# Keys of every fourth instead of every second sequence made beside the token list, sources loaded sooner, value units paced by matmul work

## The reference, cut to what matters

```python
topk_w, topk_idx = _route(x, w_router, b_router)          # 4096 tokens, 8 of 64 experts
o = ragged_dot(silu(g) * u, we_down, group_sizes)
y = zeros.at[tok].add(o * w_sorted[:, None])
...
k = keys @ Wk.T + bk;  gk = key_grid @ Wgk.T + bgk         # keys: fside_BxSxS_0, key_grid: ctx_1024
v = values @ Wv.T + bv; gv = key_grid @ Wgv.T + bgv
```

## Time and profile before

| | us |
|---|---|
| median of 3 runs (lowest, highest) | 4605.66 (4602.35, 4606.22) |
| the profiled execution, own time | 4598.36 |
| its span | 4596.7 |
| mean granted TensorE clock, share of full speed | 0.925 |
| prelude of the list (1121 to 1143) | 22 |
| list stage (1143 to 1284) | 141 |
| expert blocks (1284 to 1890) | 606 |
| gather stage of L0_ffn (1890 to 2292) | 402 |

### The profile page before, as it was taken

How to read it: one execution, slowest core, us unless ns; L and a number is a source line. 1 busy time by engine, 2 the same in 40 slices (tenths; PEclk the granted TensorE clock), 3 DMA queues, 4 the chain that set the end, 5 groups by cost and what they waited for, 6 DMA issues and landing times. The chain is left out here.

```text
span 4596.7 us, 96186 instructions
## 1 busy us (share of the span) xinstructions
PE 4050.1 (88%) x32872; PEld 3198.7 (70%) x32872; DVE 2544.2 (55%) x5993; ACT 1849.0 (40%) x3819; POOL 2193.6 (48%) x2362
## 2 busy tenths in 40 slices
PE   6999699965989999688779997999999998499992
PEld 5887577654878888566658774666666665399991
DVE  4665466568944443355546654555555555855553
ACT  2444355533423333211134443555554554155550
POOL 1110322123156666566554534666666664256665
PEclk9999899966999999888889998999999998599996
DMA  1000000001479999777700003332343341166553
GB/s 52 0 0 1 29 12 9 3 29 46 163 228 299 301 299 302 233 240 244 234 12 0 0 1 115 106 105 71 103 106 92 81 106 34 70 221 225 212 205 117
DMA packets 295001, 540.89 MB, mean 118 GB/s; under 512 B 36496, under 2 KB 136976, under 8 KB 283792
## 3 DMA queue, kind: packets, MB, share of 16 engines
q1 hardware_dynamic: 154128, 340.87, 21.5%
q0 software_dynamic: 107264, 136.38, 12.1%
q10 hardware_dynamic: 33408, 60.83, 3.5%
HBM read 380.66 MB, written 140.51 MB: 113 GB/s over the span
## 5 line engine op out<-in xcount | busy, mean ns | idle before, releaser
L1885 POOL DMA_INDIRECT L_ffn_xin<-zs,L_ffn_listed x464 | 501.1, 1080 | 282.9 <-issue 149.8
L509 POOL TENSOR_TENSOR L_xattn_p<-L_xattn_p,L_xattn_rsum 128x1024 f32<-128x1024 f32 x256 | 484.7, 1893 | 273.1 <-DVE L_xattn_rsum L578 270.6
L543 DVE TENSOR_REDUCE L_xattn_negmax<-L_xattn_scores 128x2 f32<-128x1024 f32 x256 | 313.1, 1223 | 382.0 <-PE L_xattn_scores L648 381.9
L2240 POOL DMA_INDIRECT L_ffn_back<-ys,L_ffn_slots x320 | 313.5, 980 | 191.3 <-issue 90.0
L1917 PE MATMUL L_ffn_bank<-L_ffn_xT,L_ffn_w 128*128 128x256 f32 x1536 | 367.9, 383 | 4.3 <-issue 3.2
L1151 ACT ACTIVATE L_attn_pT<-L_attn_bank 128x384 f32<-128x384 f32 x512 | 223.4, 488 | 351.0 <-PE L_attn_bank L1255 351.0
L601 ACT ACTIVATE L_xattn_p<-L_xattn_scores,L_xattn_negmax 128x512 f32<-128x512 f32 x512 | 346.0, 686 | 17.0 <-DVE L_xattn_negmax L543 16.2
L1917 PEld LDWEIGHTS L_ffn_bank<-L_ffn_xT,L_ffn_w 128*128 128x128 f32 x1536 | 278.7, 191 | 38.3 <-issue 6.6
L645 PE MATMUL L_xattn_scores<-L_xattn_kT,L_xattn_qT 64*128 64x512 f32 x1024 | 291.6, 644 | 14.0 <-ACT L_xattn_p L601 12.0
L1984 ACT ACTIVATE L_ffn_xT<-L_ffn_bank 128x512 f32<-128x512 f32 (+1 forms) x232 | 137.8, 594 | 402.5 <-DVE L_ffn_yo L2143 200.8
L607 ACT ACTIVATE L_xattn_pT<-L_xattn_turned 128x512 f32<-128x512 f32 x256 | 153.1, 598 | 336.5 <-PE L_xattn_turned L660 336.5
(11 more groups left out here) (374 smaller groups left out, 11135.1 us busy)
## 6 DMA issues: line engine op xcount, KB each, us to landing
L_ffn_w<-in_L_ffn_w SPq DMA_DIRECT2D x80, 1024.0 KB
L_ffn_w<-in_L_ffn_w SPq DMA_DIRECT2D x192, 384.0 KB
ys<-L_ffn_yo ACTq DMA_DIRECT2D x232, 256.0 KB
kv<-kv_v_row SPq DMA_DIRECT2D x128, 256.0 KB
L_xattn_mask<-in_L_xattn_mask POOLq DMA_DIRECT2D x256, 128.0 KB, 2.5
L_xattn_kT<-kv SPq DMA_DIRECT2D x16, 2048.0 KB, 9.6
L_xattn_v<-kv SPq DMA_DIRECT2D x16, 2048.0 KB, 14.9
kv<-kv_lk_row SPq DMA_DIRECT2D x64, 256.0 KB, 2.0
```

What stands on the lines that cost most here:

```text
L509: pool.tensor_tensor(p[:, s % 4, :, :], p[:, s % 4, :, :], rsum[:, s % 2, :, None].to_broadcast([P, 2, c.keys]), ALU.mult).then_inc(n_read ...
L543: dve.tensor_reduce(negmax[:, s % 2, :], s_ps[s % 2][:, :, :], AX.X, ALU.max, negate=True).then_inc(m_ready, 1)
L1885: pool.indirect_dma_start(xin[j % U][:, t, :], None, zs, bass.IndirectOffsetOnAxis(ap=listed[:, 2 * j + t:2 * j + t + 1], axis=0)).then_in ...
L2240: pool.indirect_dma_start(back[:, i % NG, :], None, ys, bass.IndirectOffsetOnAxis(ap=slots[:, tile, k:k + 1], axis=0)).then_inc(b_in[i % N ...
```

## The change

Three things are done. (1) The list stage holds the keys of every fourth sequence (3, 7, 11, 15): 32 units instead of 64, the first ahead of pick 24 and then one every 7 picks. The other 32 go to the gather stage, whose loops now run over four sequences: three with keys and values, the fourth with values alone. (2) SP loads the sources of sequence i + 2 behind the second row pair of sequence i, once the sources of sequence i are split. (3) `unit_at` spaces value units by weights: 20 for one that has a key unit beside it, 12 for one alone, which over the 240 steps makes 2.083 and 1.25 steps. POOL's splits for the list stage also wait for `owner_taken`.

```diff
     RING = 4
-    LISTED = 8 * (B // 2)
+    QUADS = B // 4
+    LISTED = 8 * QUADS
...
-                sp.dma_start(dst, self.ins[key][2 * j + 1].rearrange("(c p) s -> p c s", p=P)).then_inc(self.lx_in[j % 2], 16)
+                sp.dma_start(dst, self.ins[key][4 * j + 3].rearrange("(c p) s -> p c s", p=P)).then_inc(self.lx_in[j % 2], 16)
...
-            if g == 2 and j + 2 < B // 2:
+            if g == 2 and j + 2 < self.QUADS:
...
-    def list_pool(self, pool):
+    def list_pool(self, pool, begun):
...
+        pool.wait_ge(begun, 1)
         split_sources(0)
         split_weight(0)
         split_weight(1)
         split_sources(1)
-        for j in range(2, B // 2):
+        for j in range(2, self.QUADS):
             split_sources(j)
...
+        def keep(quad, u, last):
+            i = quad * 4 + u
...
             for g in range(8):
                 r = g % self.RING
-                if u == 0:
-                    sp.wait_ge(self.k_taken, pair * 8 + g + 1 + self.RING)
+                if u < 3:
+                    sp.wait_ge(self.k_taken, quad * 24 + u * 8 + g + 1 + self.RING)
                     sp.dma_start(out[:, g, :, :].rearrange("b p n -> p (b n)"), self.k_row[:, r, :]).then_inc(self.k_kept[r], 16)
-                sp.wait_ge(self.v_taken, pair * 16 + u * 8 + g + 1 + self.RING)
+                sp.wait_ge(self.v_taken, quad * 32 + u * 8 + g + 1 + self.RING)
                 sp.dma_start(out[:, 8 + g, :, :].rearrange("b p n -> p (b n)"), self.v_row[:, r, :]).then_inc(self.v_kept[r], 16)
+                if g == 1 and not (last and u >= 2):
+                    sp.wait_ge(self.x_split, quad * 4 + u + 1)
+                    load_sources(quad, u + 2)
...
-        load_sources(1, 1)
-        with sp.Fori(0, PAIRS - 1, 1) as pair:
-            for u in range(2):
-                keep(pair, u)
-                sp.wait_ge(self.v_made, pair * 16 + u * 8 + 8)
-                load_sources(pair * 2 + u + 2, u)
...
+        load_sources(0, 1)
+        with sp.Fori(0, self.QUADS - 1, 1) as quad:
+            for u in range(4):
+                keep(quad, u, False)
...
+        def sequence(quad, u):
+            pe.wait_ge(self.x_split, quad * 4 + u + 1)
             for g in range(8):
-                value(pair, 1, g)
+                if u < 3:
+                    key(quad, u, g)
+                value(quad, u, g)
...
+        with pe.Fori(1, self.QUADS, 1) as quad:
+            for u in range(4):
+                sequence(quad, u)
...
+        keys_at = {24 + 7 * unit: unit for unit in range(keys.LISTED)} if keys else {}
...
-                    keys.list_pool(pool)
+                    keys.list_pool(pool, owner_taken)
...
-                    if keys and i % 4 == 0:
-                        keys.list_unit(pe, i // 4)
+                    if keys and i in keys_at:
+                        keys.list_unit(pe, keys_at[i])
...
-        unit_at = {16 + unit * (len(order) - 16) // (8 * B): unit for unit in range(8 * B)}
+
+        unit_at, passed = {}, 0
+        for unit in range(8 * B):
+            unit_at[16 + passed * (len(order) - 16) // (8 * B // 4 * (3 * 20 + 12))] = unit
+            passed += 12 if unit // 8 % 4 == 3 else 20
```

90 lines of the change are left out of this document (43 added, 47 removed).

## The result

| | before | after |
|---|---|---|
| median of 6 runs (lowest, highest), us | 4602.6 (4595.7, 4606.2) | 4585.7 (4582.3, 4591.6) |
| profiled execution, own time (span) | 4598.4 (4596.7) | 4587.1 (4585.5) |
| prelude, its first operation to the first hot_low | 25.55 | 26.50 |
| list stage, first hot_low to table | 137.0 | 116.7 |
| expert blocks | 605.7 | 606.0 |

Ratio of the runs 0.9965, interval 0.9952 to 0.9978: faster by 17 us, where I had forecast 40. The parts of the profiled executions add up: +1.0 - 20.3 + 0.3 + 6.7 = -12.3, and the spans differ by 11.2. The list stage did what was forecast, the gather stage did the opposite: +6.7 us instead of -23. The total of 4585.7 lies inside the range of the forecast, but it came about in another way than my own case has it.

The account below looks back on a forecast made before the run. TensorE was taken to pace the list stage; in the gather stage TensorE, GpSimd and DMA limits lay close, with most loss in waits. -19.0 + 1.6 - 23 = -40 gave 4564 us, range 4528 to 4596.

Parts of the forecast that it names:

- my own case: Whole kernel: list stage, start and gather stage together save 40 us, median 4605.7 to about 4565; chance 0.53.
- List stage, -19.0: List stage: with 32 key units gone VectorE becomes the bound, 117.6 us instead of 136.6.
- Start, +1.6: Prelude: waiting for `owner_taken`, four operations each wait out one split, so the list starts 1.6 us later; bounds -6 to +5.
- the prices worked out by it: Port-lock reading of the skill: a list cycle with splits costs 2.5 us rather than 1.93, the start near +5.
- Gather stage, -23: Gather stage: -40.8 from TensorE's and GpSimd's paces, +18 for slow phases; bounds -63 to +17.
- the slow phases: Gather stage: late first values, 6 us at each of three places where values alone precede keys, +18 in all.
- The waits for sources: Gather stage: VectorE's stops at source splits (4.57 us in one case) vanish, loads going out some 20 us ahead.
- The rival that came true: Gather stage stands still, more units eating what earlier loads give; only the list gains: 4588 us, chance 0.15.
- Slow phases go with the uneven pace: Gather stage: PE's pace keeps GpSimd near its 16 buffers, so slow phases end early: -80 in all, 4526, chance 0.22.
- the DMA engines at 243 GB/s: Gather stage moves its bytes at 243 GB/s at best: 428 us, +26, with the list +9, 4615; chance 0.03.
- At most four gaps of PE of more than 4 us: Gather stage: a sign expected in the profile after, limiting TensorE's long gaps to four.
- PE stays at 1.2 GHz: List stage: TensorE at half clock makes it 190 us instead of 137, +30 in all, 4636; chance 0.02.

Follow-up runs that it names:

- e15: The changed kernel run again, word for word, in the last group: gather stage 421.3 us, total 4610.8 against 4615.7 before, ratio 0.9987.
- e1: Changed kernel, but GpSimd issues only the first 16 gathers of the gather stage: stage 325.8 us, total 4503.3 against 4602.2 before.
- e2: Changed kernel, but each gather of the stage is a plain load of 128 consecutive rows: stage 329.5 us, total 4503.7 against 4602.2 before.
- e9: Changed kernel with two of every four gathers issued behind the first 16: stage 329.1 us, total 4515.9 against 4613.8 before.
- e18: Changed kernel with gather-stage key units of 2 matmuls instead of 12, last group: stage 399.8 us, total 4597.3 against 4615.7 before.
- e11: Changed kernel with gather-stage value units as 12 matmuls of 256 columns instead of 6 of 512: stage 434.6 us, total 4617.4 against 4613.8 before.
- e5: Kernel before the change with only the first 16 gathers of the gather stage: stage 286.6 us, total 4495.1 against 4603.1 before.
- e7: Changed kernel with sources loaded behind the sequence as before and list splits not waiting for the prelude's end: stage 412.5 us, ratio to before 0.9971.
- e8: Changed kernel with the loops of SyncE, TensorE and ScalarE written out: stage 406.9 us, total 4587.9, ratio to before 0.9970.
- e6: Changed kernel with the old even spacing, a value unit every 1.875 steps: stage 413.9 us, ratio to before 0.9975.
- e10: Changed kernel with gather-stage key units as 6 matmuls of 512 columns instead of 12 of 256: stage 402.4 us, total 4592.2 against 4613.8 before.
- e14: Changed kernel, GpSimd at most 4 gathers ahead in the first 48 steps, in the group without the loss: stage 343.3 us, ratio to before 0.9973.
- e13: Changed kernel with gather-stage key units of 2 matmuls instead of 12, in the group without the loss: stage 333.9 us, total 4505.8 against 4523.4 before.
- e16: Changed kernel, GpSimd at most 4 gathers ahead in the first 48 steps, last group: stage 424.2 us, ratio to before 0.9992.

## Why the prediction was right or wrong

**List stage, -19.0: right.** Measured -20.3: 116.7 against the 117.6 of the sum, tiles 3.46 apart, two cycles of 5.35 for splits, TensorE's clock no matter. What the sum lacked is the case of e15, where GpSimd is kept out for 22.8 us. Before the change VectorE waited 0.62 us in every cycle, which may have let it in; but VectorE without gaps is not enough for the case, as 14 traces show it without gaps and the split at 2.1 us.

**Start, +1.6: right in kind.** +0.95, with the four waits at the places named. The Trainium skill (SBUF — State Buffer, the section on the two sides of SBUF) has each of the two engines wait out the other's operation on their shared port pair; these rows agree in kind, but the prices worked out by it, near +5 for the start and 2.5 us for a cycle beside splits, were too high: +0.95 and 1.9 (5.35 - 3.46).

**Gather stage, -23: wrong, +6.7.** The arithmetic of TensorE's work was right: e1 shows 22.2 us for eight pairs and a stage of 326. The step that failed is the one in front of it: "From there 11 sequences with keys cost 8 x 2.78 = 22.2 each", with GpSimd at 1.25 us for a gather beside it, and the slow phases as three extras of 6 us. Measured, the 11 took 273 us instead of 245, and the 4 without keys 67 instead of 50: 340 where the sum had 295, or 313 with its 18 for slow phases. The loss is not tied to the change of sequences: it goes with the gathers (e1, e2, e9), and this balance of work leaves GpSimd little rest, 256 gathers at 1.25 being 320 us and the stage without gathers 326. Where the loss occurs, the stage takes 1.56 to 1.70 us for a gather, with far less effect of TensorE's work than the forecast had: 401 us with 192 units, 408 and 421 with 224, 400 with short keys (e18), 435 with more instructions (e11). So before the change neither TensorE's work nor the sources were what held the stage: without the gathers it took 287 us instead of 401 (e5), and relieving them could not shorten it.

**The waits for sources.** I had counted that the stops for sources vanish. They did: in the changed kernel VectorE doesn't wait at a split. But e5 shows that without gathers they were 4 us in all, and e7 that with gathers they are worth about 5 (412.5 against 406.9 of e8 in its group). A stop there may have given GpSimd the rest that it now takes elsewhere; that is argued, not shown.

**The rival that came true** is the one that had the stage stand still and the list alone gain (4588 us, given 0.15), though not for its reason, earlier loads that more units eat up. Its chance was too low: the trace held TensorE's gaps without a releaser in mid-unit, and VectorE's waits that end when GpSimd stops, in both kinds of sequence, and the forecast treated them as a remainder of 18 us. "Slow phases go with the uneven pace" falls with e6; "the DMA engines at 243 GB/s" with e2, at 314.

**What was to show it.** List: held. Start: held. Pairs 2.78 apart: between the stumbles, yes. "At most four gaps of PE of more than 4 us": none behind the start-up, but 22 of over 1 us, and with the clock at 0.91 TensorE is busy for 344 us with what takes 314 in e1. One sum of a rival has a slip: "PE stays at 1.2 GHz" counts 36.6 groups where there are 32 units; by its own prices the stage would take 177 us, not 190.

**Open.** Which path GpSimd's gathers block was not found; e11 speaks for a part played by TensorE's count of instructions, e10 hardly does. TensorE runs at full pace beside 8 us of gathers without a stop (2000 to 2008), so a lack of rest alone isn't the whole condition. Nor is it known why one group is free of the loss, and whether the scattered rows or the recording take part. No version here beats the changed kernel by more than the intervals allow.

## What to carry to other kernels

When several engines each show idle time and none is near its limit, take one of them out of the stage in a throwaway kernel before pricing anything: one run without gathers would have shown that 287 of the stage's 401 us were the other engines' work, and that 114 came with the gathers, partly GpSimd's own 320 us, partly disturbance. Work moved into such a stage was nearly free here (32 units for 7 us), and waits removed from it were worth nearly nothing. A small gain should be measured in more than one group of runs: the ratio of this change was 0.9965 in one and 0.9987 in another.

## What the runs showed of the hardware

- Beside GpSimd's gathers, at 0.95 us and 0.30 us apart, the other engines are held up in four of the five groups: TensorE's matmuls come 0.7 to 1.4 us apart instead of 0.12, a signal reaches VectorE 4.4 us late, and in the changed kernel 36 of 128 signals are recorded on time. With half of the gathers this is nearly gone (329 us against 326 with 16 of them); in the group of e14 it is gone with all of them.
- GpSimd's own pace sets the stage where nothing is held up: 256 gathers, 343 us (e14), 334 with 111 us less of TensorE's work (e13).
- The DMA engines carried 314 GB/s at a share of 0.92 in e2, beside TensorE at its full rate, which is more than the 254 GB/s that the disturbed stage reached. For 34 us it was 388, with TensorE busy all the time at a clock of 1.00 (e2, view of stretches):
```profile
1912.00:1946.00 34.00, 34.00 (x216) 30.79 (x215) 24.37 (x49) 12.87 (x30) 17.68 (x33) 1.00 1.04 388
```
The Trainium skill (DMA: Bandwidth & Descriptors, "Where 436 GB/s comes from") has about 358 GB/s as the limit of the HBM side. This row lies above it, so the 356 of the earlier trace rows, which the forecast took to agree with it, were no limit.
- The same kernel (before) took 4523 us in one group of runs and 4602 to 4616 in the others. By the changed kernel's variants the gather stage makes most of the difference (343 us in e14, 424 in e16); the expert blocks took 597 us there, 606 and 615 elsewhere.
- A GpSimd operation of 1.3 us can be kept waiting for 22 us beside a VectorE that runs short operations without a gap (e15 to e18); in 14 other traces with such a VectorE it took 2.1 us. The Trainium skill (SBUF — State Buffer, the section on the two sides of SBUF) has it that the loser of the shared port pair "fully blocks", for one instruction of the other. This row goes further: the wait lasts over six tiles of nine instructions each.
